# Two attentions of a transformer kernel: turns, weighing, key side and copies put in new orders

## The chip, the cores and the metric

The kernel runs on one core of one Trainium2 chip. The metric is device time in microseconds (us) for one execution, median of several runs. TensorE multiplies matrices into PSUM banks (eight, of 128 x 512 fp32), VectorE and ScalarE work on PSUM and SBUF, and SyncE (SP) issues all transfers, in one list.

## The reference

Two layers on x of 8 x 512 x 128 (8 sequences, 512 positions, 128 channels), 16 heads of width 8, so 128 heads of 512 x 512 scores in each attention:

```python
# layer 0: attention with relative positions at both sides
scores = einsum(Q, K) * scale + take(einsum(Q, pos_key) * scale, rel_pos) + swap(take(einsum(K, pos_query) * scale, p2c_pos))
ctx = softmax(scores) @ V;  x = layernorm(x + ctx @ Wo.T + bo)
# layer 0: gated feed-forward with a one-step shift; x = layernorm(x + ...)
# layer 1: attention with shifted sinusoid positions
scores = (Q K^T + u K^T + rel_shift(Q r^T + v r^T)) / sqrt(dk)
ctx = softmax(scores) @ V;  x = layernorm(x + ctx @ Wo + bo)
# layer 1: feed-forward 128 -> 512 -> 512 -> 512 -> 128; x = layernorm(x + ...)
```

## The kernel before

The program has five stages, one after the other with small overlaps: an opening that makes stacked queries, keys and values; the first attention (`rel` is true); a mixing stage; the second attention (`rel` is false); a closing stage with the last feed-forward.

In both attentions the work goes head by head. The order on each engine is written out by hand; nothing is planned at run time. A step works on head j's turns and, ahead of it, on scores, exponentials and corrections of later heads. Eight steps are unrolled in a loop; the first four and the last steps stand outside. Four heads are a group. The pieces of a step, four of each kind, one for each tile of 128 queries (or, for turns, keys):

- S, `score_tile` (L821 to L827), TensorE: a score tile of 128 x 512, 6 tiles ahead in the first attention, 7 in the second. It waits until the exponential has emptied its bank (four score banks). In the first attention a last small part goes to a shared bank `other` and waits for the mask M of the tile before.
- T, `turn` (L842), TensorE: four transposes of the head's exponentials into a bank. In the first attention turns 0 and 3 use bank 5, which the key side also uses, and turns 1 and 2 use bank 6, which the correction also uses; in the second they alternate.
- W, `weigh` (L855), TensorE: sums of values for the group before, for one quarter of the keys, four matmuls over the whole width of 512. Its first quarter waits for the copies of all four heads and for the copy of the group before out of the bank `cbank`.
- K, `key_side` (L741), TensorE, first attention: the key-side product for head j+7, which needs that head's stack `a_stks`. C, `correction` (L748, L749): for head j+5. In the second attention `edge` (L722) for head j+5 instead.
- M, `mix` (L908), F, `finish` (L920), X, `row_max` (L928), VectorE: mask (first attention only), added band, and negated maximum of a tile. `key_out` (L755) copies K's result, `edge_out` (L933) that of the edge.
- E, `exp_tile` (L980), P, `copy_turned` (L987), ScalarE: exponential of a tile (4 tiles ahead in the first attention, 5 in the second), and the copy of a turn. `corr_out` (L761) copies the correction, `group_out` (L993) the summed group, in one step of four.
- SyncE, `sync_step`: for each head of the first attention the key side is written to a DRAM buffer (L634) and read back skewed (L640), the correction likewise (L646, L652), and the stack of head j+8 is loaded in two transfers (L608, L609), in the order L634, L646, L652, L608, L609, L640. In the last step of a group come after L609 a table and offsets (L621, L628, L629), and at the end the store of the group and a load of values (L671, L673).

The orders before, by engine:

```
first attention    TensorE  S T W  S T K  S T  S T C
                   VectorE  M X F  M X F key_out  M X F  M X F
                   ScalarE  E P  E P (group_out)  E P  E P corr_out
second attention   TensorE  S T W  S T edge  S T  S T
                   VectorE  F X  F X  F X  F X edge_out
                   ScalarE  E P  E P (group_out)  E P  E P
```

Of the kernel before, what the change touches and what calls it, by code (L numbers as in the profile page):

```python
# [21 lines left out]
B, T, C = 8, 512, 128  # L22
H = 16
DH = C // H
NT = T // 128
NHEAD = B * H
# [38 lines left out]
def build(nc, t):  # L65

    top = ExitStack()
    with top:
# [430 lines left out]
        def attention(layer):  # L499
# [289 lines left out]
            def program(block, before, after):  # L789
# [56 lines left out]
                def weigh(pe, h, k):  # L846
# [15 lines left out]
                def tensor_step(pe, i, j, left, weighed=True):  # L862
                    own = Head(i, j)
                    for k in range(NT):
                        if left >= (k + score_ahead) // NT:
                            score_tile(pe, *ahead(i, j, k, score_ahead))
                        turn(pe, own, k)
                        if k == 0 and weighed:
                            weigh(pe, Head(i, j - j % GROUP - GROUP), j % GROUP)
                        if not rel and k == 1 and left >= CORR_AHEAD:  # L870
                            pe.wait_ge(corr_copied, BASE + own.n + CORR_AHEAD)
                            edge(pe, Head(i, j + CORR_AHEAD), corr_bank)
                        if rel and k == 1 and left >= KEY_AHEAD:
                            pe.wait_ge(copied, BASE + 4 * own.n + 1)
                            key_side(pe, Head(i, j + KEY_AHEAD), key_bank)
                    if rel and left >= CORR_AHEAD:
                        pe.wait_ge(copied, BASE + 4 * own.n + 3)
                        correction(pe, Head(i, j + CORR_AHEAD))

                @block.tensor  # L880
                def _(pe):
# [16 lines left out]
                    for k in range(NT):  # L898
                        weigh(pe, Head(loops, FIRST + last - GROUP), k)
# [34 lines left out]

                @block.vector
                def _(v):
# [11 lines left out]
                    def vector_step(i, j, left):  # L948
                        for k in range(NT):

                            if left >= (k + score_ahead) // NT:
                                if rel:
                                    mix(v, *ahead(i, j, k, score_ahead))
                                else:
                                    finish(v, *ahead(i, j, k, score_ahead))
                            if left >= (k + score_ahead - 1) // NT:
                                row_max(v, *ahead(i, j, k, score_ahead - 1))
                            if rel and left >= (k + score_ahead) // NT:
                                finish(v, *ahead(i, j, k, score_ahead))
                            if not rel and k == 3 and left >= CORR_AHEAD:  # L960
                                edge_out(v, Head(i, j + CORR_AHEAD))
                            if rel and k == 1 and left >= KEY_AHEAD:
                                key_out(v, Head(i, j + KEY_AHEAD), key_bank)

                    for j in range(FIRST):
                        vector_step(0, j, NHEAD)
# [3 lines left out]
                    for j in range(last):  # L970
                        vector_step(loops, FIRST + j, last - 1 - j)
                        after.vector_tail(v, last - 1 - j)

# [22 lines left out]
                def _(act):  # L996
# [3 lines left out]
                    def scalar_step(i, j, left, weighed=True):  # L1000
                        own = Head(i, j)
                        for k in range(NT):
# [1032 lines left out]
```

## Time and profile before

| | |
|---|---|
| median of 3 runs | 1965.22 us (1956.04 to 1966.07) |
| profiled execution | 1965.38 us, its span 1963.2 us |
| granted clock of TensorE, mean | 0.961 |
| TensorE, VectorE, ScalarE busy | 88%, 74%, 75% of the span |
| transfers | 404.44 MB, mean 206 GB/s |
| first attention | about 97 to 860 us |
| second attention | about 1040 to 1640 us |

All times of the trace are us from the start of the span. TensorE's weight loads (PEld) overlap its matmuls (PE). An instruction's duration overlaps the start of the next one on the same engine by about 0.1 us, so the distance of two starts is the slot that one takes.

### The profile page before, as it was taken

To read this page: it belongs to the slowest core of one execution; us is meant where nothing else is said; L and a number is where in the kernel's file an instruction comes from. 1 tells how busy PE (TensorE), PEld (TensorE's weight loads), DVE (VectorE), ACT (ScalarE), POOL (GpSimd) and SP (SyncE) were. 2 spreads that over 40 slices of the span, in tenths; PEclk is the share of its full clock that TensorE was granted. 3 is DMA by queue.
4 is the path that set the end of the run, shared out by engine and by line. 5 is a ranking of instruction groups with operands and counts; after the bars stand their busy time and mean duration, and the time that the engine had idled before them with its cause. 6 is when DMAs were issued, how large, how long until landed. Compare 5 with 4: busy or idle time off the path is not lost.

```text
span 1963.2 us, 44049 instructions
## 1 busy us (share of the span) xinstructions
PE 1728.0 (88%) x11694; PEld 1040.9 (53%) x11694; DVE 1446.4 (74%) x3501; ACT 1475.8 (75%) x2605; POOL 80.2 (4%) x102
## 2 busy tenths in 40 slices
PE   5479999999999999977767999999999989999998
PEld 2145555555555555545444655655666544545454
DVE  5568888888888888876977888888888873244322
ACT  4458888888888888876878999999999974232221
POOL 0000000000000000003520000000000000000000
PEclk8679999999999999998978999999999989999999
DMA  6788888888888888865999777777777771001000
GB/s 207 281 249 256 268 265 261 263 263 266 264 266 265 264 259 264 259 183 158 342 338 297 217 213 210 213 212 214 210 214 213 209 211 44 21 27 37 21 6 11
DMA packets 414359, 404.44 MB, mean 206 GB/s; under 512 B 36969, under 2 KB 334561, under 8 KB 414177
## 3 DMA queue, kind: packets, MB, share of 16 engines
q1 hardware_dynamic: 414305, 403.80, 67.3%
q8 instruction: 24, 0.39, 0.1%
q14 instruction: 30, 0.25, 0.0%
HBM read 226.89 MB, written 176.30 MB: 205 GB/s over the span
## 4 chain that ended last, share of the span: by engine, by line
PE 48%; issue 13%; ACT 11%; DVE 9%; SPq 8%; DMA 6%; POOL 0%; DVEq 0%; ACTq 0%; POOLq 0%
PE bank L842 12%; PE bank L1847 11%; PE bank L855 9%; ACT a_probt L987 5%; PE bank L821 4%; DVE a_negmax L928 3%; DMA a_stks<-stack 3%; ACT a_prob L980 3%; DVE a_keyside L755 2%; DVE bank L908 2%; PE bank L823 2%; PE bank L1839 1%; PE bank L1840 1%; PE bank L1868 1%; PE bank L722 1%
## 5 line engine op out<-in xcount | busy, mean ns | idle before, releaser
L980 ACT ACTIVATE a_prob<-bank,a_negmax 128x512 f32<-128x512 f32 x1024 | 738.2, 721 | 44.7 <-DVE a_negmax L928 43.2
L928 DVE TENSOR_REDUCE a_negmax<-bank 128x1 f32<-128x512 f32 x1024 | 698.3, 682 | 0.2 <-issue 0.2
L842 PE MATMUL bank<-ident,a_prob 128*128 128x128 f32 x4096 | 646.5, 281 | 56.8 <-ACT a_probt L987 49.0
L987 ACT COPY a_probt<-bank 128x512 f32<-128x512 f32 x1024 | 619.5, 605 | 97.4 <-PE bank L842 85.6
L842 PEld LDWEIGHTS bank<-ident,a_prob 128*128 128x128 f32 x4096 | 451.5, 142 | 174.9 <-issue 70.7
L920 DVE TENSOR_TENSOR bank<-bank,a_band 128x128 f32<-128x128 f32 (+3 forms) x1024 | 349.5, 341 | 81.6 <-PE bank L823 66.5
L821 PE MATMUL bank<-a_stks 74*128 74x192 bf16 (+7 forms) x1024 | 324.9, 317 | 31.5 <-ACT a_prob L980 29.4
L855 PE MATMUL bank<-a_probt,a_vs 128*32 128x512 f32 x2048 | 275.3, 612 | 12.8 <-ACT a_probt L987 12.8
L821 PEld LDWEIGHTS bank<-a_stks 74*128 74x128 bf16 (+1 forms) x1024 | 100.2, 98 | 260.0 <-ACT a_prob L980 215.0
L908 DVE COPY_PREDICATED bank<-a_mask,bank 128x128 f32<-128x128 uint32 (+1 forms) x512 | 139.4, 272 | 112.0 <-PE bank L827 109.7
L823 PE MATMUL bank<-a_stks 74*128 74x320 bf16 (+5 forms) x768 | 201.8, 263 | 0.0
L1913 DVE TENSOR_TENSOR d_drop<-bank,d_s 128x128 f32<-128x128 f32 x32 | 7.1, 283 | 170.4 <-PE bank L1868 170.4
L748 PE MATMUL bank<-ident,a_sheared 128*128 128x128 f32 x512 | 106.5, 285 | 19.4 <-DMA a_sheared<-shear_a 15.0
L827 PE MATMUL bank<-a_stks 74*128 74x128 bf16 (+1 forms) x512 | 110.4, 216 | 10.9 <-DVE bank L908 2.7
L1847 PE MATMUL bank<-d_ha,d_h1T 128*128 128x512 f32 x256 | 112.3, 592 | 0.0
L1847 PE MATMUL bank<-d_hb,d_h2T 128*128 128x512 f32 x256 | 111.2, 592 | 0.0
L755 DVE COPY a_keyside<-bank 128x512 f32<-128x512 f32 x128 | 87.2, 681 | 24.8 <-PE bank L741 24.4
L749 PE MATMUL bank<-a_tabs,a_stks 65*128 65x128 bf16 x512 | 97.5, 225 | 0.0
L761 ACT COPY a_corr<-bank 128x512 f32<-128x512 f32 x128 | 76.4, 597 | 23.2 <-DMA shear_b<-a_corr 11.9
L748 PEld LDWEIGHTS bank<-ident,a_sheared 128*128 128x128 f32 x512 | 74.3, 145 | 34.7 <-issue 21.5
L1898 ACT ACTIVATE d_hb<-bank,d_fs 128x512 f32<-128x512 f32 x32 | 22.0, 687 | 90.6 <-PE bank L1847 90.6
L1903 ACT ACTIVATE d_hc<-bank,d_fs 128x512 f32<-128x512 f32 x32 | 22.0, 687 | 87.6 <-PE bank L1847 87.6
(178 smaller groups left out, 1622.7 us busy)
## 6 DMA issues: line engine op xcount, KB each, us to landing
a_band<-shear_b SPq DMA_DIRECT2D x128, 512.0 KB, 4.9
shear_a<-a_keyside SPq DMA_DIRECT2D x128, 256.0 KB, 3.7
a_sheared<-shear_a SPq DMA_DIRECT2D x128, 256.0 KB, 3.7
shear_b<-a_corr SPq DMA_DIRECT2D x128, 256.0 KB, 2.8
shear_e<-a_corr SPq DMA_DIRECT2D x128, 256.0 KB, 2.2
a_band<-shear_e SPq DMA_DIRECT2D x128, 256.0 KB, 3.1
a_stks<-stack SPq DMA_DIRECT2D x256, 96.0 KB, 3.0
a_stks<-stack SPq DMA_DIRECT2D x384, 48.0 KB, 2.5
```

The costliest lines, as they stand in the source:

```text
L748: pe.matmul(corr_bank[:, q], sheared[h.slot % 4][:, q], ident[:, :], is_transpose=True, start=True, stop=False)
L755: v.tensor_copy(keyside[h.slot % 4][:, :], source[:, :]).then_inc(key_copied, 1)
L821: last = pe.matmul(score[:, 0:c], k[:, qlo, q], k[:, keys, 0:c], start=True, stop=True)
L823: last = pe.matmul(score[:, c:T], k[:, qhi, q], k[:, keys, c:T], start=True, stop=True)
L842: last = pe.transpose(turned_bank[k][:, n * 128:(n + 1) * 128], prob[h.slot % 2][:, n, k * 128:(k + 1) * 128], ident[:, :])
L855: pe.matmul(cbank[32 * j:32 * j + VW, :], vs[g][:, at:at + VW], probt[h.slot + j][:, k, :], start=(k == 0), stop=(k == NT - 1)).then_inc(p ...
L908: v.copy_predicated(score[:, a:e], mask[:, 0:e - a], other[:, 0:e - a]).then_inc(fixed, 1)
L920: v.tensor_tensor(score[:, a:e], score[:, a:e], band[h.slot % bands][:, n, w:w + e - a], ALU.add).then_inc(added, 1)
L928: v.tensor_reduce(negmax[h.slot % 2][:, n:n + 1], score[:, :], AX.X, ALU.max, negate=True).then_inc(maxed, 1)
L980: nc.scalar.activation(prob[h.slot % 2][:, n, :], score[:, :], ACT.Exp, bias=negmax[h.slot % 2][:, n:n + 1]).then_inc(exped, 1)
L987: nc.scalar.copy(probt[h.slot][:, k, :], turned_bank[k][:, :]).then_inc(copied, 1)
L1847: last = pe.matmul(dst[:, :], w[:, k, 128 * m:128 * m + 128], src[:, k, :], start=(k == 0), stop=(k == KH - 1))
```

## The change

Both attentions get orders of their own in place of a loop over the four pieces. By engine:

```
first attention    TensorE  S T  S T K W  T S  T S C
                   VectorE  M X  M F F X key_out X  M F  M X F
                   ScalarE  P E  P E E  P E  P (group_out) corr_out
second attention   TensorE  S T T  S W S  T T  S edge
                   VectorE  F X  F X (group copy)  F X  F X edge_out
                   ScalarE  E P P E  E P P E
```

The copy of the summed group in the second attention moves from ScalarE to VectorE. `weigh` gets an argument for columns, which always is the whole width. SyncE's list is not changed. The core of the diff (the VectorE and ScalarE orders in it are those of the lines above):

```diff
-                def weigh(pe, h, k):
+                def weigh(pe, h, k, cols):
...
-                        pe.matmul(cbank[32 * j:32 * j + VW, :], vs[g][:, at:at + VW], probt[h.slot + j][:, k, :],
-                                  start=(k == 0), stop=(k == NT - 1)).then_inc(pv_mm, 1)
+                        part = pe.matmul(cbank[32 * j:32 * j + VW, cols], vs[g][:, at:at + VW], probt[h.slot + j][:, k, cols],
+                                         start=(k == 0), stop=(k == NT - 1 and cols.stop == T))
+                        if cols.stop == T:
+                            part.then_inc(pv_mm, 1)
...
+                def shifted_tensor_step(pe, i, j, left, weighed=True):
                     own = Head(i, j)
-                    for k in range(NT):
-                        if left >= (k + score_ahead) // NT:
-                            score_tile(pe, *ahead(i, j, k, score_ahead))
-                        turn(pe, own, k)
-                        if k == 0 and weighed:
-                            weigh(pe, Head(i, j - j % GROUP - GROUP), j % GROUP)
-                        if not rel and k == 1 and left >= CORR_AHEAD:
-                            pe.wait_ge(corr_copied, BASE + own.n + CORR_AHEAD)
-                            edge(pe, Head(i, j + CORR_AHEAD), corr_bank)
-                        if rel and k == 1 and left >= KEY_AHEAD:
-                            pe.wait_ge(copied, BASE + 4 * own.n + 1)
-                            key_side(pe, Head(i, j + KEY_AHEAD), key_bank)
-                    if rel and left >= CORR_AHEAD:
+                    score_ahead_of(pe, i, j, left, 0)
+                    turn(pe, own, 0)
+                    score_ahead_of(pe, i, j, left, 1)
+                    turn(pe, own, 1)
+                    if left >= KEY_AHEAD:
+                        pe.wait_ge(copied, BASE + 4 * own.n + 1)
+                        key_side(pe, Head(i, j + KEY_AHEAD), key_bank)
+                    if weighed:
+                        weigh(pe, Head(i, j - j % GROUP - GROUP), j % GROUP, slice(0, T))
+                    turn(pe, own, 2)
+                    score_ahead_of(pe, i, j, left, 2)
+                    turn(pe, own, 3)
+                    score_ahead_of(pe, i, j, left, 3)
+                    if left >= CORR_AHEAD:
                         pe.wait_ge(copied, BASE + 4 * own.n + 3)
                         correction(pe, Head(i, j + CORR_AHEAD))
+
+                def edged_tensor_step(pe, i, j, left, weighed=True):
+                    own = Head(i, j)
+                    score_ahead_of(pe, i, j, left, 0)
+                    turn(pe, own, 0)
+                    turn(pe, own, 1)
+                    score_ahead_of(pe, i, j, left, 1)
+                    if weighed:
+                        weigh(pe, Head(i, j - j % GROUP - GROUP), j % GROUP, slice(0, T))
+                    score_ahead_of(pe, i, j, left, 2)
+                    turn(pe, own, 2)
+                    turn(pe, own, 3)
+                    score_ahead_of(pe, i, j, left, 3)
+                    if left >= CORR_AHEAD:
+                        pe.wait_ge(corr_copied, BASE + own.n + CORR_AHEAD)
+                        edge(pe, Head(i, j + CORR_AHEAD), corr_bank)
...
+                def edge_group_out(v, h):
+
+                    v.wait_ge(pv_mm, BASE + 16 * (h.use(GROUP) + 1))
+                    v.wait_ge(out_written, BASE + 16 * h.use(GROUP))
+                    v.tensor_copy(outs[:, :], cbank[:, :]).then_inc(out_copied, 1)
...
-                    group_out(act, Head(loops, FIRST + last - GROUP))
+                    if rel:
+                        group_out(act, Head(loops, FIRST + last - GROUP))
```

## Rows read from the trace of the kernel before

**Rows 1.** Busy time by stretch: us, busy (x instructions) by engine, PEclk, DMA share, GB/s.

```profile
500.00:700.00 200.00, 186.50 (x1481) 115.63 (x1480) 170.43 (x438) 173.85 (x312) 0.00 (x0) 1.00 0.86 263
...
1300.00:1500.00 200.00, 188.34 (x1561) 119.49 (x1558) 176.67 (x403) 196.63 (x368) 0.00 (x0) 1.00 0.73 212
```

**Rows 2.** Waits, 200 to 800 us: who waited for whom, us in total, times, longest.

```profile
PE bank L741 <- DMA a_stks<-stack: 6.2, 10, 1.2
```

**Rows 3.** Timeline, one step of the first attention: start, us, engine, line, tiles, idle before.

```profile
201.84 0.63 PE L842 MATMUL bank<-ident,a_prob 128*128 128x128 f32 x4 [0.18 <-ACT a_probt L987]
...
202.40 1.06 PE L855 MATMUL bank<-a_probt,a_vs 128*32 128x512 f32 x8
...
203.39 0.39 PE L821 MATMUL bank<-a_stks 74*128 74x512 bf16 x1
...
203.65 0.63 PE L842 MATMUL bank<-ident,a_prob 128*128 128x128 f32 x4
...
203.96 0.23 DVE L908 COPY_PREDICATED bank<-a_mask,bank 128x64 f32<-128x64 uint32 x1 [0.92 <-PE bank L827]
...
204.12 0.38 PE L741 MATMUL bank<-a_stks,a_tabs 65*128 65x512 bf16 x1
...
204.20 0.35 SPq L609 DMA_DIRECT2D a_stks<-stack  x1
...
204.96 0.68 DVE L755 COPY a_keyside<-bank 128x512 f32<-128x512 f32 x1
...
206.48 0.27 PE L748 MATMUL bank<-ident,a_sheared 128*128 128x128 f32 x1
...
207.17 0.35 PE L821 MATMUL bank<-a_stks 74*128 74x448 bf16 x1
...
207.78 0.63 PE L842 MATMUL bank<-ident,a_prob 128*128 128x128 f32 x4 [0.18 <-ACT a_probt L987]
```

**Rows 4.** Timeline, copies of the summed groups in the first attention (L993).

```profile
162.29 0.59 ACT L993 COPY a_outs<-bank 128x512 f32<-128x512 f32 x1
...
786.04 0.59 ACT L993 COPY a_outs<-bank 128x512 f32<-128x512 f32 x1
...
809.82 0.59 ACT L993 COPY a_outs<-bank 128x512 f32<-128x512 f32 x1
...
834.53 0.59 ACT L993 COPY a_outs<-bank 128x512 f32<-128x512 f32 x1
```

**Rows 5.** Chain of waits after 216 us, and the instruction it ends in.

```profile
217.15 5.13 DMA a_stks<-stack
...
222.40 0.39 PE L741 MATMUL bank<-a_stks,a_tabs 65*128 65x512 bf16 x1 [0.27 <-DMA a_stks<-stack]
```

**Rows 6.** Transfers issued at 312.7, 337.9 and 792.4 us (L609): count, KB, us to landing.

```profile
a_stks<-stack SPq DMA_DIRECT2D x1, 48.0 KB, 6.1
...
a_stks<-stack SPq DMA_DIRECT2D x1, 48.0 KB, 3.6
...
a_stks<-stack SPq DMA_DIRECT2D x1, 48.0 KB, 5.0
```

**Rows 7.** Timeline, second attention: ScalarE's pair of copy and exponential, group copies, weighing.

```profile
1108.43 0.78 ACT L980 ACTIVATE a_prob<-bank,a_negmax 128x512 f32<-128x512 f32 x1
...
1109.02 0.67 ACT L987 COPY a_probt<-bank 128x512 f32<-128x512 f32 x1
...
1109.48 0.80 ACT L980 ACTIVATE a_prob<-bank,a_negmax 128x512 f32<-128x512 f32 x1
...
1114.88 0.63 ACT L993 COPY a_outs<-bank 128x512 f32<-128x512 f32 x1
...
1117.78 1.07 PE L855 MATMUL bank<-a_probt,a_vs 128*32 128x512 f32 x8 [0.44 <-ACT a_probt L987]
...
1132.89 0.63 ACT L993 COPY a_outs<-bank 128x512 f32<-128x512 f32 x1
...
1150.81 0.63 ACT L993 COPY a_outs<-bank 128x512 f32<-128x512 f32 x1
```

More of the change, by code:

```diff
@@ L898, in _ @@
                     for k in range(NT):
-                        weigh(pe, Head(loops, FIRST + last - GROUP), k)
+                        weigh(pe, Head(loops, FIRST + last - GROUP), k, slice(0, T))
                 def mix(v, h, n):
@@ L946, in _, with mix_ahead_of @@
                             row_max(v, *ahead(0, 0, 0, n - 1))
[L948 to L963, printed above, removed]
+                    def mix_ahead_of(i, j, left, k):
+                        if left >= (k + score_ahead) // NT:
+                            mix(v, *ahead(i, j, k, score_ahead))
@@ new lines, in edged_vector_step @@
+                    def edged_vector_step(i, j, left, weighed=True):
+                        finish_ahead_of(i, j, left, 0)
+                        max_ahead_of(i, j, left, 0)
+                        finish_ahead_of(i, j, left, 1)
+                        max_ahead_of(i, j, left, 1)
+                        if weighed and j % GROUP == GROUP - 1:
+                            edge_group_out(v, Head(i, j - j % GROUP - GROUP))
+                        finish_ahead_of(i, j, left, 2)
+                        max_ahead_of(i, j, left, 2)
+                        finish_ahead_of(i, j, left, 3)
+                        max_ahead_of(i, j, left, 3)
+                        if left >= CORR_AHEAD:
+                            edge_out(v, Head(i, j + CORR_AHEAD))
@@ L972, in _ @@
                         after.vector_tail(v, last - 1 - j)
+                    if not rel:
+                        edge_group_out(v, Head(loops, FIRST + last - GROUP))
                 def exp_tile(act, h, n):
@@ L998, in _, with exp_ahead_of, shifted_scalar_step, edged_scalar_step @@
                         exp_tile(act, *ahead(0, 0, 0, n))
[L1000 removed]
+                    def exp_ahead_of(i, j, left, k):
+                        if left >= (k + exp_ahead) // NT:
+                            exp_tile(act, *ahead(i, j, k, exp_ahead))
+                    def shifted_scalar_step(i, j, left, weighed=True):
                         own = Head(i, j)
[L1002 to L1009 removed]
+                        copy_turned(act, own, 0)
+                        exp_ahead_of(i, j, left, 0)
+                        copy_turned(act, own, 1)
+                        exp_ahead_of(i, j, left, 1)
+                        exp_ahead_of(i, j, left, 2)
+                        copy_turned(act, own, 2)
+                        exp_ahead_of(i, j, left, 3)
+                        copy_turned(act, own, 3)
+                        if weighed and j % GROUP == GROUP - 1:
+                            group_out(act, Head(i, j - j % GROUP - GROUP))
+                        if left >= CORR_AHEAD:
+                            corr_out(act, Head(i, j + CORR_AHEAD))
+                    def edged_scalar_step(i, j, left, weighed=True):
+                        own = Head(i, j)
+                        exp_ahead_of(i, j, left, 0)
+                        copy_turned(act, own, 0)
+                        copy_turned(act, own, 1)
+                        exp_ahead_of(i, j, left, 1)
+                        exp_ahead_of(i, j, left, 2)
+                        copy_turned(act, own, 2)
+                        copy_turned(act, own, 3)
+                        exp_ahead_of(i, j, left, 3)
+                    scalar_step = shifted_scalar_step if rel else edged_scalar_step
                     for j in range(FIRST):
```

35 lines of the change are left out of this document (27 added, 8 removed).

## The prediction

> **What bounds the kernel now.** I read the busy shares by stretch first: they show two long regular stretches, the two attentions, and a last stretch that the change does not touch. In the first attention no engine is full: TensorE 93%, VectorE 85%, ScalarE 87%, DMA 86%, at a granted clock of 1.00 [rows 1]. In the second ScalarE is full: 196.6 of 200 us [rows 1]. Next the waits, for what closes the first attention's loop: now and then TensorE's key-side product waits for a load of the head's stack (10 times, 6.2 us) [rows 2]. Then one step by the timeline, 201.84 to 207.78: 5.94 us [rows 3]. The loop in it: turn 0 at 201.84, the weighing at 202.40, and only then the score tile at 203.39; VectorE sat idle 0.92 us for that tile's end (mask at 203.96), so its key-side copy starts at 204.96 though the key-side product started at 204.12 and took 0.38 us; the fourth tile's last part, the fourth turn, its copy and the next turn 0 (207.78, released by a copy, 0.18 us idle) follow from there. The 1 us of weighing stands where VectorE has nothing to do.
>
> Groups of four heads take more than 4 x 5.94 = 23.8 us: 24.01 on average (162.29 to 834.53, 28 groups), the last two 23.78 and 24.71 [rows 4]. The chain says what the excess is: after a group step SyncE is behind. The stack load is issued at 217.15, 9.37 us after the group step's turn 0 (207.78), lands 5.13 us later, and the key-side product of the step after the next starts at 222.40, released by it [rows 3, 5]. In such a step that product stands 2.28 us after turn 0, so it may start at 2 x 5.94 + 2.28 = 14.2 us; the load landed at 14.5.
>
> **The first attention, part by part.** Nothing is removed; TensorE's order becomes S T S T K W T S T S C. Its own pace from the rows [rows 3]: a turn followed by a small product 0.47 (203.65 to 204.12), four of them 1.9; the weighing 0.99 (202.40 to 203.39); the correction 0.69 (206.48 to 207.17); the four tiles 0.26 (203.39 to 203.65) to 0.35 each, 1.3; the key side 0.2 to 0.3. Sum 5.15 to 5.25. Now each wait, with t = 0 at turn 0. Turn 0 ends 0.65, its copy (0.59, now first on ScalarE) ends 1.28, so K goes at 1.33. W at 1.55 to 2.54, where ScalarE copies the second turn (ends 2.35) and VectorE does mask, maximum and band of two tiles: the wait of 0.92 is covered. VectorE: K's copy after the third of its pieces starts 2.5 and ends 3.2; turn 3 wants it at 3.36. The masks M2 and M3 follow S2 and S3 (about 3.7 and 4.5), the maximum after them ends 5.3, before the exponential that needs it at 5.9. The band add F2 now stands directly behind its own mask M2 and waits for its completion: 0.1 us, in a gap before S3 ends, so nothing. ScalarE: copy, exp, copy, exp, exp, copy, exp, copy, correction copy; 4 x 0.59 + 5 x 0.46 = 4.7 us (the slots of 1108.43 to 1109.02 and 1109.02 to 1109.48) [rows 7], with the last turn's copy ending at 5.1; the next turn 0 can start at 5.2. The group copy, moved from the second turn to the step's end, pushes the correction's copy by 0.46 in one step of four and the next turn 1 by 0.1. So all three engines allow about 5.27 us, 21.1 us a group against 23.8: 0.67 us a head.
>
> What is late next is the load. K moves from 2.28 to 1.33 us after turn 0, and the steps are shorter. What queues behind its wait on TensorE is W, both remaining turns, S2, S3 and C: everything. SyncE's list is untouched, and in the group step it runs without a pause (correction copy, then band, two stack loads, table, offsets, store, values): the load of the following step is issued 9.4 us after the group step's turn 0 in the new order too. Its landing took 5.1, 6.1, 3.6 and 5.0 us in four groups [rows 5, 6], mean 4.95. K may start at 2 x 5.27 + 1.33 = 11.9, the load is there at 9.4 + 4.95 = 14.35: a stall of 2.45 us a group (bounds: 1.1 with 3.6, 3.6 with 6.1). Nothing catches it up. Group: 21.1 + 2.45 = 23.55 against 24.01, 0.46 less; some 30 groups: **14 us** off. The gain's ends: 0.67 x 120 = 80 us plus the old stalls' 7 if landings shrink to nothing that binds, and below nothing in the last rival. I take 14 since landing times are measured and SyncE's order stays.
> In a plain step the load is issued 2.36 us after turn 0 (204.20) [rows 3] and K of the next step wants it at 5.27 + 1.33 = 6.6: 4.2 us for a landing. That holds with 3.6, not with 5.1; after the stall there is 2.5 us of slack, so I count nothing.
>
> On landing times the Trainium skill (DMA: Bandwidth & Descriptors, "Anatomy of one DMA") gives, as a fit for transfers of the other descriptor path, about 2.0 us plus bytes over 436 GB/s. The trace does not agree for this load: 3.6 to 6.1 us with DMA 86% busy [rows 1, 6]. By that fit 48 KB would be there in 2.1 us, K would never wait, and the total would come out as in the first rival.
>
> **The second attention.** ScalarE makes a pair of exponential and copy in 1.05 us (1108.43 to 1109.48), 4.2 a step, plus the group's copy, another slot of 0.46 [rows 7]. Groups take 18.01 (1114.88 to 1132.89) and 17.92 (1132.89 to 1150.81) [rows 7]: 4 x 4.22 = 16.9, 0.5 for the copy, 0.6 for a hole. The hole: the group's copy delays the next turn's copies, the weighing that needs them waits 0.44 (1117.78) [rows 7] with everything behind it. The change takes the group's copy from ScalarE and gives it to VectorE, after the weighing's new place. VectorE's busy time goes from 88% of 4.49 us [rows 1] = 3.97 to 3.97 + 0.68/4 = 4.1 us a step: below 4.22. In the group step its copy (0.6) pushes the next mask-free add and maximum; an exponential then comes 0.15 to 0.2 us late. TensorE: busy at most 94% of 4.49 = 4.23 [rows 1], with modelled ends; turn, turn, tile, weighing, tile, turn, turn, tile, edge leaves it 4.0 to 4.1. The weighing now has two turns and a tile between itself and the last copy it waits for, so the 0.44 goes. Pairs E E and P P do not stand in the trace; I take the sum of the two slots, 1.05, as in an alternating pair; if each had the copy's or the exponential's slot it would be 0.92 or 1.18. The last exponential of a step writes the buffer that turn 3 reads, and now stands behind both copies, so that wait is over. Group: 16.9 + 0.2 = 17.1 against 17.97, 0.87 less; about 30 groups: **26 us** (ends: 0 and 36, the latter with no late exponential and no hole).
>
> The `cols` argument always holds the whole width: no cost. The last group's copy goes to VectorE, beside other work: 0.7 us at most.
>
> Sum against the profiled execution, 1965.38 us (span 1963.2, 2.2 around it; the median of the three runs is 1965.22, so both stand alike): 1965.4 - 14 - 26 = 1925. I forecast **1925 us**, its own range 1900 to 1945.
>
> **Rivals.** First, the loads land in time: DMA queues less where it is drained evenly. For it: half the groups have no stall now (23.78) [rows 4]. Against it: 86% of 24.0 us is 20.6 us of DMA work a group, in 21.1 us. Time: 1965.4 - 78 - 26 = 1861.
> Second, the loads take the whole gain of the first attention: stall 2.9 us a group, which landings of 5.4 us would make (5.1 and 6.1 were seen, and DMA is denser). Only the second attention gains: 1939.
> Third, neither gains: in the second attention two turns back to back cost more than a turn and a tile (no row shows them; 0.63 us each, the duration of one, instead of 0.45 brings TensorE to 4.5 us a step), and the first is as in the second rival. Time 1965.
> Fourth, the other side. The plain steps too wait for their load: with K at 1.33, a step is as long as issue and landing allow, 2.36 + L - 1.33. With L = 4.0 it is 5.03 and does not bind; with 5.13 it is 6.16, more than today's 6.00. Slower in total by over 10 us needs 6.3 us, so L of 5.3 or more in every step; at 5.4 it is 6.43: 0.43 x 120 = 52 later, 26 gained, 1991. For it: SyncE issues nothing earlier and DMA fills up. Against it: a longer step empties the queue again.
>
> **How the numbers follow.** Forecast 0.52; loads in time 0.10; second attention alone 0.16; neither 0.12; every step waits 0.10. Against 0.5% (10 us, about what a measurement of this kernel can tell from no change): faster 0.52 + 0.10 + 0.16 = 0.78, same 0.12, slower 0.10. The range runs from 1868, which leaves out half of the first rival and more, to 1966, which leaves out the last: 0.82 inside.
>
> **What would show it.** In the changed profile: VectorE's wait for the tile behind the weighing (0.92) gone; plain steps of 5.2 to 5.4 us between turn 0s; TensorE's key side waiting for the stack load in nearly every group, 1 to 4 us, in total 50 to 90 us; group copies 22.5 to 24.5 us apart. In the second attention no 0.44 before the weighing, ScalarE still over 97% busy, groups 17.0 to 17.3 us apart, with VectorE's copy of the sums in them. It is wrong if plain steps stay at 5.9 (then a walk of mine missed a wait), if the key side hardly waits, or if TensorE's steps in the second attention exceed 4.3 us.

## The result

The changed kernel takes 1975.49 us (median of 20 runs, 1962.34 to 1993.38), the kernel before 1962.03 us (20 runs, 1955.85 to 1968.74): the ratio is 1.0074, 95% interval 1.0057 to 1.009. It is slower by about 14 us where 1925 was forecast, and outside the range. In the experiments below a ratio is always to the kernel before, measured beside it on the same chip. "Groups" are the mean distance of two copies of a summed group, in us. A group step is the step of each four in which the group's copy stands; the stalled step is the second one behind it; the others are called plain.

The profiled execution took 1989.61 us (span 1987.8, mean granted clock 0.931) against 1965.38 (1963.2, 0.961), 24.6 us more of span. This execution is one of the slower ones, 14 us above the median of the 20, so the losses read from its trace are at the upper end. In the 20 runs the time follows the granted clock: 1962.34 us at 0.946, 1975.06 at 0.939, 1993.38 at 0.930. By landmarks: the last copy of a correction in the first attention moved from 856.1 to 889.2, so 33.1 us are lost up to there; 4.4 more are lost before the second attention; the second attention wins 13.3 back; the end loses 0.4.

The busy times by stretch, changed kernel (us, then busy time and instructions of TensorE (PE), its weight loads (PEld), VectorE (DVE), ScalarE (ACT) and POOL, then granted clock, DMA share, GB/s), answer to [rows 1]:

```profile
500.00:700.00 200.00, 181.29 (x1396) 115.40 (x1395) 163.78 (x414) 161.69 (x295) 0.00 (x0) 0.91 0.82 250
...
1300.00:1500.00 200.00, 196.19 (x1607) 120.67 (x1605) 186.10 (x423) 196.84 (x368) 0.00 (x0) 1.00 0.76 218
```

In the first attention every engine did less in 200 us than before, and the clock is 0.91 where it was 1.00. The second has its old clock and did more in its 200 us. ScalarE is 98% busy there, as before.

The copies of the summed groups, changed kernel, first attention (ScalarE) and second (VectorE), the first and the 29th of 32, and the second and the 27th of 32, answer to [rows 4, 7]:

```profile
168.33 0.60 ACT L1057 COPY a_outs<-bank 128x512 f32<-128x512 f32 x1
...
868.59 0.61 ACT L1057 COPY a_outs<-bank 128x512 f32<-128x512 f32 x1
```

```profile
1134.30 0.69 DVE L965 COPY a_outs<-bank 128x512 f32<-128x512 f32 x1
...
1570.89 0.69 DVE L965 COPY a_outs<-bank 128x512 f32<-128x512 f32 x1
```

A group takes (868.59 - 168.33) / 28 = 25.01 us in the first attention (before 24.01), and (1570.89 - 1134.30) / 25 = 17.46 us in the second (before 17.97).

The waits of the key-side product, 200 to 800 us, changed kernel (who waited for whom, us in total, times, longest), answer to [rows 2]:

```profile
PEld bank L741 <- issue: 50.4, 27, 3.5
...
PE bank L741 <- DMA a_stks<-stack: 34.9, 13, 3.2
```

A row for the weight load and a row for the matmul: they overlap, and the first counts at least once for each of the 24 groups in the window. Before, the same two rows had 15 waits of 10.5 us in all (longest 1.4) and 10 of 6.2 (longest 1.2). Some rows name a copy or "issue" in place of the load; there too the load lands just as the wait ends (351.89 + 4.3 us for the key side at 356.26, 403.07 + 4.3 for the one at 407.49). The chain of waits runs through the same load (start, us, what), as in [rows 5]:

```profile
427.60 5.18 DMA a_stks<-stack
...
432.91 0.61 PE bank L741
...
433.52 1.87 PE bank L855 x8
```

The weighing is the line to look at: its row says 1.87 us. The timeline (start, us, engine, line, operation, idle time before) of the same kernel, at a stalled step (330.47), at two plain steps (349.23, 399.89), at a second stalled step (403.87 to 409.76) and at a third (784.48), answers to [rows 3]:

```profile
330.47 0.61 PE L741 MATMUL bank<-a_stks,a_tabs 65*128 65x512 bf16 x1 [3.22 <-DMA a_stks<-stack]
...
331.01 1.94 PE L855 MATMUL bank<-a_probt,a_vs 128*32 128x512 f32 x8
...
349.23 0.39 PE L741 MATMUL bank<-a_stks,a_tabs 65*128 65x512 bf16 x1 [0.57 <-DMA a_stks<-stack]
...
349.57 1.06 PE L855 MATMUL bank<-a_probt,a_vs 128*32 128x512 f32 x8
...
399.89 0.39 PE L741 MATMUL bank<-a_stks,a_tabs 65*128 65x512 bf16 x1
...
400.22 1.06 PE L855 MATMUL bank<-a_probt,a_vs 128*32 128x512 f32 x8
...
403.07 0.35 SPq L609 DMA_DIRECT2D a_stks<-stack  x1
...
403.87 0.61 PE L842 MATMUL bank<-ident,a_prob 128*128 128x128 f32 x4
...
407.49 0.48 PE L741 MATMUL bank<-a_stks,a_tabs 65*128 65x512 bf16 x1 [2.21 <-issue]
...
407.89 1.94 PE L855 MATMUL bank<-a_probt,a_vs 128*32 128x512 f32 x8
...
409.76 1.12 PE L842 MATMUL bank<-ident,a_prob 128*128 128x128 f32 x4
...
784.48 0.39 PE L741 MATMUL bank<-a_stks,a_tabs 65*128 65x512 bf16 x1 [2.78 <-DMA a_stks<-stack]
...
784.79 1.07 PE L855 MATMUL bank<-a_probt,a_vs 128*32 128x512 f32 x8
```

Directly behind a wait of 3.22 or 2.21 us the weighing (L855) takes 1.94 us; behind none, or 0.57 us, it takes 1.06. The turn behind it at 409.76 takes 1.12 instead of 0.66, as at 401.22 in the step before. But behind a wait of 2.78 us, at 784.48, the weighing takes 1.07 too. The granted clock, read in half microseconds over 200 to 800 us, falls during or behind 20 of the 24 stalls, for 3.5 to 7 us each, and stays at 1.00 at four. The shortest wait with a fall is 1.53 us, the longest without one 2.78, so the length of the wait alone does not decide. The granted clock in the three pieces around the stall at 407.49:

```profile
401.00:406.00 5.00, 4.28 (x39) 3.16 (x35) 4.72 (x13) 4.60 (x9) 0.00 (x0) 1.00 0.95 277
...
407.50:411.00 3.50, 3.50 (x15) 1.41 (x16) 1.29 (x2) 0.08 (x1) 0.00 (x0) 0.52 0.99 293
...
411.00:413.00 2.00, 2.00 (x22) 1.66 (x20) 1.44 (x5) 1.64 (x4) 0.00 (x0) 0.99 0.41 155
```

It is 1.00 (2.4 GHz) ahead of the stall, 0.52 (1.2 GHz) in the 3.5 us of dense work behind it, 0.99 after that.

In the second attention two waits are new or larger (1100 to 1600 us, changed kernel): VectorE's band add waits for its transfer, and an exponential waits for a maximum.

```profile
DVE bank L946 <- DMA a_band<-shear_e: 16.7, 28, 2.4
...
ACT a_prob L1044 <- DVE a_negmax L954: 12.9, 21, 2.4
```

One such place, behind a group step: SyncE issues the read of the band, VectorE wants it, it is late, and an exponential is late behind it.

```profile
1264.89 0.38 SPq L665 DMA_DIRECT2D a_band<-shear_e  x1
...
1268.64 0.82 ACT L1044 ACTIVATE a_prob<-bank,a_negmax 128x512 f32<-128x512 f32 x1
...
1269.26 0.30 DVE L946 TENSOR_TENSOR bank<-bank,a_band 128x128 f32<-128x128 f32 x1 [0.99 <-DMA a_band<-shear_e]
...
1270.19 0.69 ACT L1044 ACTIVATE a_prob<-bank,a_negmax 128x512 f32<-128x512 f32 x1 [0.72 <-DVE a_negmax L954]
```

### The profile page after: what moved, and what is told of

Its sections match the earlier page's. It is cut to its first block, busy times and chain, and to the rows that moved or that the text cites. A ratio compares the mean times of both kernels' runs of the same rounds, so it can differ in the third digit from the quotient of the medians.

```text
span 1987.8 us, 44062 instructions
## 1 busy us (share of the span) xinstructions
PE 1747.4 (88%) x11694; PEld 1054.3 (53%) x11694; DVE 1472.9 (74%) x3533; ACT 1450.3 (73%) x2573; POOL 80.0 (4%) x102
## 4 chain that ended last, share of the span: by engine, by line
PE 53%; SPq 15%; DMA 12%; issue 8%; DVE 6%; ACT 5%; POOL 0%; DVEq 0%; ACTq 0%; POOLq 0%
PE bank L842 14%; PE bank L1934 11%; PE bank L855 8%; DMA a_band<-shear_e 5%; PE bank L821 4%; DMA a_stks<-stack 4%; PE bank L748 3%; PE bank L823 2%; DVE a_negmax L954 2%; PE bank L741 2%; ACT a_probt L1051 1%; PE bank L1926 1%; PE bank L1927 1%; PE bank L1955 1%; PE bank L827 1%
## 5 line engine op out<-in xcount | busy, mean ns | idle before, releaser
L1044 ACT ACTIVATE a_prob<-bank,a_negmax 128x512 f32<-128x512 f32 x1024 | 699.3, 738 | 33.8 <-DVE a_negmax L954 32.5
L1051 ACT COPY a_probt<-bank 128x512 f32<-128x512 f32 x1024 | 595.6, 629 | 123.7 <-PE bank L842 117.6
L842 PE MATMUL bank<-ident,a_prob 128*128 128x128 f32 x4096 | 619.5, 286 | 12.8 <-ACT a_probt L1051 10.0
L842 PEld LDWEIGHTS bank<-ident,a_prob 128*128 128x128 f32 x4096 | 459.3, 145 | 185.4 <-ACT a_probt L1051 89.9
L946 DVE TENSOR_TENSOR bank<-bank,a_band 128x128 f32<-128x128 f32 (+3 forms) x1024 | 340.5, 344 | 71.7 <-DMA a_band<-shear_e 25.9
L821 PE MATMUL bank<-a_stks 74*128 74x192 bf16 (+7 forms) x1024 | 329.9, 322 | 33.9 <-ACT a_prob L1044 30.3
L855 PE MATMUL bank<-a_probt,a_vs 128*32 128x512 f32 x2048 | 290.2, 642 | 0.8 <-ACT a_probt L1051 0.4
L748 PE MATMUL bank<-ident,a_sheared 128*128 128x128 f32 x512 | 113.2, 298 | 23.2 <-DMA a_sheared<-shear_a 18.3
L741 PE MATMUL bank<-a_stks,a_tabs 65*128 65x512 bf16 x128 | 53.4, 417 | 84.8 <-DMA a_stks<-stack 39.6
L827 PEld LDWEIGHTS bank<-a_stks 74*128 74x128 bf16 x512 | 51.3, 100 | 76.4 <-DVE bank L934 53.0
```

Of the source, the lines that this page charges most:

```text
L748: pe.matmul(corr_bank[:, q], sheared[h.slot % 4][:, q], ident[:, :], is_transpose=True, start=True, stop=False)
L821: last = pe.matmul(score[:, 0:c], k[:, qlo, q], k[:, keys, 0:c], start=True, stop=True)
L827: last = pe.matmul(other[:, 0:e - a], k[:, qhi, q], k[:, keys, a:e], start=True, stop=True)
L842: last = pe.transpose(turned_bank[k][:, n * 128:(n + 1) * 128], prob[h.slot % 2][:, n, k * 128:(k + 1) * 128], ident[:, :])
L855: part = pe.matmul(cbank[32 * j:32 * j + VW, cols], vs[g][:, at:at + VW], probt[h.slot + j][:, k, cols], start=(k == 0), stop=(k == NT - 1 ...
L946: v.tensor_tensor(score[:, a:e], score[:, a:e], band[h.slot % bands][:, n, w:w + e - a], ALU.add).then_inc(added, 1)
```

## The experiments

Two theories stood against each other for the first attention: that the stall at the key side costs its own length and slows the clock behind it, and that the new orders are in themselves no faster (a wait that the prediction's walk through the step missed). For the second attention the rivals were ScalarE's new order and the late band.

### Each attention alone

e1_second_only has the old orders in the first attention, e2_first_only in the second:

```diff
-tensor_step = shifted_tensor_step if rel else edged_tensor_step
+tensor_step = old_tensor_step if rel else edged_tensor_step       # e1
+tensor_step = shifted_tensor_step if rel else old_tensor_step     # e2
 # likewise vector_step and scalar_step; the second attention's group copy follows its orders
```

> Old orders in the first attention, new orders in the second alone. Theory: the first attention of the changed kernel is what costs; in its profile the second attention's groups are 17.5 us apart instead of 17.97, so this kernel should be some 13 to 15 us faster than before (about 1948 us). Rival: the second attention's gain is lost at its ends or needs the first one's, then within 5 us of before (1962).

> New orders in the first attention alone, old ones in the second. Theory: groups of the first attention 25.1 us apart instead of 24.0, plus the slower start: 25 to 35 us slower than before (about 1990 us), granted clock in that stretch near 0.90. Rival: the loss sits in the second attention or between the two, then about 1962.

e1: 1951.16 us, ratio 0.9946 (0.9933 to 0.9959), groups 23.91 and 17.45 us. e2: 1991.66 us, 1.0157 (1.0141 to 1.0172), groups 24.69 and 17.97, mean clock 0.939. So the second attention gives about 10 us, somewhat less than the 13 to 15 expected, and the first costs about 30, as expected, though at a clock of 0.95 in its stretch where 0.90 was expected. Their product, 1.010, is a little above the 1.0074 of both together. The changed kernel's own runs lie 31 us apart, those of before 13. As time and clock go together in those runs, a number of falls that differs from run to run would make such a spread (20 in the trace above, 15 in e2's over the same 600 us); this was not tested. e2's stretch:

```profile
300.00:500.00 200.00, 180.53 (x1431) 114.00 (x1431) 168.37 (x424) 166.88 (x303) 0.00 (x0) 0.95 0.86 262
```

### The load of the stack at the top of SyncE's list

```diff
                 if rel:
+                    if left >= LOAD_AHEAD:
+                        hold(sp, maxed, 4 * (n + 1))
+                        head_load(sp, Head(i, j + LOAD_AHEAD))
                     if left >= CORR_AHEAD + 1:
                         shear_a_write(sp, Head(i, j + CORR_AHEAD + 1))
...
-                    if left >= LOAD_AHEAD:
-                        hold(sp, maxed, 4 * (n + 1))
-                        head_load(sp, Head(i, j + LOAD_AHEAD))
```

> The changed kernel with one edit: SyncE issues the two stack loads at the top of each step of the first attention instead of behind the band read. Theory (the key side waits for the load after each group step, and the clock falls behind that wait): the load of the step behind a group step is issued about 2.5 us earlier, the stall of 2 to 3 us goes to under 1, the clock stays at 1.00, groups of 21.5 to 22.5 us; about 75 to 100 us faster than the changed kernel, 1880 to 1900 us. Rival (the transfers as a whole are the limit, whichever comes first): another transfer, the band or the sheared key side, is late instead and the groups stay at 24 us or more, 1950 us or more.

e3 is the changed kernel with this edit, e10 the kernel before with it.

> The kernel before with old orders everywhere and one edit: the stack loads at the top of SyncE's step in the first attention. Theory (the old order was bound by its own loop through the weighing, and the late load cost only 0.3 us a group): 5 to 12 us faster than before, 1950 to 1957 us, groups of 23.7 us. Rival (the late load was the bound already and the new orders add nothing of their own): 1900 us or less.

e3: 1893.5 us, 0.9653 (0.9637 to 0.967). e10: 1957.54 us, 0.9976 (0.9965 to 0.9988), groups 23.76. e3's stretch and its first and last group copy of the first attention:

```profile
300.00:500.00 200.00, 195.72 (x1637) 125.95 (x1632) 191.42 (x484) 188.01 (x345) 0.00 (x0) 1.00 0.94 293
```

```profile
167.40 0.61 ACT L1057 COPY a_outs<-bank 128x512 f32<-128x512 f32 x1
...
771.94 0.62 ACT L1057 COPY a_outs<-bank 128x512 f32<-128x512 f32 x1
```

The clock is 1.00, DMA is at 0.94, and a group takes 604.54 / 28 = 21.59 us; the forecast without a stall was 21.1. e3's time is in the range expected, e10's gain of 5 us at the low end of it. So the new orders do nearly what the walk said once the stack load is on time. What is left, 0.49 us a group, has a candidate in e3's trace (200 to 750 us, 25 groups): the correction waits for the key side that is read back, 0.38 us a group.

```profile
PE bank L748 <- DMA a_sheared<-shear_a: 9.5, 18, 1.1
```

The first attention alone: new orders without the earlier load cost 30 us (e2), the earlier load without new orders gives 5 (e10), both give 58 (e3's 68 less the second attention's 10). Neither part shows what they are worth together.

### The same stall, with the engine kept at work

e4 adds two products of 128 x 512 into the key side's bank, ahead of the key side, in the step that stalls. Nothing reads them. All waits stay.

```diff
                         pe.wait_ge(copied, BASE + 4 * own.n + 1)
+                        if weighed and own.slot % GROUP == 1:
+                            for _ in range(2):
+                                pe.matmul(key_bank[:, :], ident[:, :], probt[own.slot][:, 0, :], start=True, stop=True)
                         key_side(pe, Head(i, j + KEY_AHEAD), key_bank)
```

> The changed kernel with two products added ahead of the key side in the one step of four that waits for its load; their results are overwritten at once. They add 1.7 us of TensorE work inside a wait of 2 to 4 us. Theory (a long wait of TensorE lowers its clock, and the steps behind it run at 1.2 GHz for some us): the weighing behind the key side takes 1.06 us instead of 1.94, granted clock of the stretch 0.97 or more, 30 to 45 us faster than the changed kernel, about 1935 to 1945 us. Rival (the wait alone costs, the clock's fall is no consequence of it): no change or up to 10 us slower where the wait is shorter than the added work, 1975 to 1985 us.

e4: 1948.02 us, 0.9942 (0.9924 to 0.9961), groups 23.58. The two products, the key side and the weighing of such a step (timeline, TensorE), and the stretch:

```profile
317.04 1.98 PE L879 MATMUL bank<-a_probt,ident 128*128 128x512 f32 x4
...
320.39 0.39 PE L741 MATMUL bank<-a_stks,a_tabs 65*128 65x512 bf16 x1 [1.37 <-DMA a_stks<-stack]
...
320.71 1.07 PE L855 MATMUL bank<-a_probt,a_vs 128*32 128x512 f32 x8
```

```profile
300.00:500.00 200.00, 194.88 (x1545) 121.42 (x1542) 176.58 (x449) 174.56 (x318) 0.00 (x0) 1.00 0.88 268
```

TensorE is given 1.98 us of useless work a group, the key side still waits 1.37 us for its transfer, and the kernel is some 27 us faster than the changed one, a little short of the 30 to 45 expected. The weighing is back at 1.07 us behind every such wait, and the clock does not fall once between 150 and 760 us. The load lands no sooner (4.1 us after its issue in the median, 4.0 in the changed kernel). This takes the length of the stall and the clock apart: 23.58 is close to what the forecast had for the stall alone (23.55), and of the 1.4 us above it in the changed kernel all but some tenths are the clock's. The tenths may be a longer wait: the changed kernel's 24 stalls average 2.3 us, and 23.58 is 2.0 above e3's 21.59.

### The weighing ahead of the key side

```diff
                     turn(pe, own, 1)
+                    if weighed:
+                        weigh(pe, Head(i, j - j % GROUP - GROUP), j % GROUP, slice(0, T))
                     if left >= KEY_AHEAD:
                         pe.wait_ge(copied, BASE + 4 * own.n + 1)
                         key_side(pe, Head(i, j + KEY_AHEAD), key_bank)
-                    if weighed:
-                        weigh(pe, Head(i, j - j % GROUP - GROUP), j % GROUP, slice(0, T))
```

> The changed kernel with one edit: in the first attention the weighing stands before the key side instead of behind it. Theory (the key side waits for a load that comes 2 to 3 us late in one step of four, and everything queued behind it waits): the weighing's 1.0 us fills the wait, the stall goes to 1 to 2 us, the clock mostly stays up; groups of 22.5 to 23.5 us instead of 25.1, about 1905 to 1930 us. Rival (the key side's copy, now late for turn 3, costs 0.3 us or more in every step): groups of 23.5 us or more, 1935 us or more.

e7: 1932.69 us, 0.9835 (0.9814 to 0.9855), groups 23.10, clock 1.00 from 300 to 700 us and two falls before that. The groups are in the range expected, the time is 3 us above it. The order takes the place of part of the stall, but in every step turn 3 now waits for VectorE's copy of the key side, and an exponential for its maximum (200 to 750 us):

```profile
PEld bank L842 <- DVE a_keyside L755: 35.3, 96, 0.4
...
ACT a_prob L1044 <- DVE a_negmax L954: 24.3, 96, 0.4
```

Some 0.37 and 0.25 us a step. With the late load this order is 43 us faster than the change's; with the load on time it was not run, and these waits speak for the change's order there.

### The second attention

e5 has the old orders in the first attention, keeps the new orders of TensorE and VectorE in the second, and lets ScalarE alternate there again; it is to be compared with e1:

```diff
-    exp_ahead_of(i, j, left, 0)
-    copy_turned(act, own, 0)
-    copy_turned(act, own, 1)
-    exp_ahead_of(i, j, left, 1)
... 
+    for k in range(NT):
+        exp_ahead_of(i, j, left, k)
+        copy_turned(act, own, k)
```

> Old orders in the first attention; in the second the new orders of TensorE and VectorE with the group copy on VectorE, but ScalarE alternating exponential and copy as before. Compare with the second attention alone (1951 us, groups 17.5 us). Theory (two exponentials back to back take 0.66 us each, an alternating pair 1.05, so ScalarE's new order costs 0.16 us a step and ScalarE is the bound): groups of 17.0 to 17.2 us, about 1940 us. Rival (VectorE or TensorE sets the 17.5): groups stay at 17.4 to 17.6, 1950 us.

e5: 1975.03 us, 1.0052 (1.0036 to 1.0069), groups 18.35 in the second attention. Neither the expectation nor its rival came true. With two turns back to back the next pair waits for a copy that the alternating order gives late (timeline, TensorE, e5):

```profile
1221.12 0.66 PE L843 MATMUL bank<-ident,a_prob 128*128 128x128 f32 x4 [0.35 <-ACT a_probt L1088]
...
1225.58 0.66 PE L843 MATMUL bank<-ident,a_prob 128*128 128x128 f32 x4 [0.28 <-ACT a_probt L1088]
```

ScalarE's paired slots were never dear (timeline, ScalarE, e1; x2 is two instructions back to back):

```profile
1218.67 1.29 ACT L1081 ACTIVATE a_prob<-bank,a_negmax 128x512 f32<-128x512 f32 x2
...
1219.82 1.10 ACT L1088 COPY a_probt<-bank 128x512 f32<-128x512 f32 x2
...
1220.76 1.33 ACT L1081 ACTIVATE a_prob<-bank,a_negmax 128x512 f32<-128x512 f32 x2
```

From 1218.67 to 1220.76 are two exponentials and two copies: 2.09 us, 1.045 a pair, where the forecast took 1.05.

e6 is the kernel before with nothing but the group copy on VectorE in the second attention, e8 is e3's first attention with e6's second.

> The kernel before with one edit: in the second attention the group copy is on VectorE, behind the maximum of the second piece; all orders old. Theory (the copy's slot on ScalarE and the hole behind it were all there was to win; ScalarE is full): groups of 17.0 to 17.2 us instead of 17.97, about 1938 us, faster than all new orders of the second attention (1951). Rival (the hole of 0.44 us before the weighing needs the weighing's new place): groups of 17.4 to 17.6, about 1950 us.

> First attention as changed with the stack loads at the top of SyncE's step (1893.5 us with the new second attention); second attention with old orders and the group copy on VectorE. Theory, as for the group copy alone: 10 to 13 us less than 1893.5, so 1880 to 1884 us. Rival, as there: 1893 us.

e6: 1962.06 us, 0.9997 (0.9986 to 1.0007), groups 17.88. e8: 1903.5 us, 0.9697 (0.9679 to 0.9716), about 10 us behind e3. Both expectations fell. In e6 the slot leaves ScalarE, and the hole stays:

```profile
1223.62 0.68 DVE L984 COPY a_outs<-bank 128x512 f32<-128x512 f32 x1
...
1225.21 0.69 ACT L1081 ACTIVATE a_prob<-bank,a_negmax 128x512 f32<-128x512 f32 x1 [0.27 <-DVE a_negmax L973]
...
1226.52 1.06 PE L856 MATMUL bank<-a_probt,a_vs 128*32 128x512 f32 x8 [0.80 <-ACT a_probt L1088]
```

VectorE's copy delays a maximum, the exponential 0.27 us, and the weighing waits 0.80 us for a turn's copy. So the copy's new engine alone does not take the hole away. In the changed kernel, where the weighing has its new place as well, no weighing waits for a turn's copy (1100 to 1600 us); no run moves the weighing alone.

e9 and e11 ask whether the late band can be had earlier by reading it ahead of the next write; e9 on top of e3, e11 with the stack's load behind L634 instead of at the top.

```diff
                 else:
-                    if left >= CORR_AHEAD:
-                        edge_write(sp, Head(i, j + CORR_AHEAD))
...
                         edge_read(sp, Head(i, j + CORR_AHEAD - 1))
+                    if left >= CORR_AHEAD:
+                        edge_write(sp, Head(i, j + CORR_AHEAD))
```

> The changed kernel with the stack loads at the top of SyncE's step in the first attention (1893.5 us) and, in the second, the skewed band read ahead of the edge write in SyncE's step, so that it no longer stands behind the wait for the edge copy. Theory (the second attention's 17.5 us instead of the 17.1 forecast are the band add that waits for this read in or after a group step, and the exponential behind it): no wait of VectorE for the band read, groups of 16.9 to 17.2 us, 8 to 14 us less, about 1882 us. Rival (the group copy on VectorE alone makes exponentials late): groups stay at 17.4 or more, 1890 us or more.

> As the load at the top with the band read first, but the stack loads stand behind the key side's write, so that write is no longer 1 us later. Theory: the load of the step behind a group step is issued 0.6 us later than at the top, its slack shrinks from about 1 us to 0.5, some groups stall by less than 1 us, the clock stays at 1.00: within 8 us of the load at the top, on either side. Rival (a threshold of the clock is met again): 15 us or more slower than the load at the top.

e9: 1903.35 us, 0.9693 (0.9673 to 0.9712), groups 21.57 and 17.89. e11: 1908.77 us, 0.9728 (0.9698 to 0.9757), groups 22.01 and 17.88. e9 missed: from 1100 to 1500 us the band is waited for 41 times, 20.6 us, in place of e3's 24 times, 11.0 us. SyncE now waits for the write's landing, and the write of the next head stands behind that read (e9):

```profile
SPq L598 <- DMA shear_e<-a_corr: 38.6, 65, 1.5
```

e11 is 5 us behind e9, the kernel that it differs from by the load alone, and 15 behind e3, where the expectation allowed 8 and its rival began at 15; 10 of them e9 has too. Its correction waits 17.1 us for the key side that is read back (200 to 750 us; e9 10.7), and its clock falls once, during such a wait of 2.03 us that ends at 355.07, in a group of 26.05 us.

e12 leaves the order of write and read, and issues every other group's store and load of values one step later, behind the band's read, in place of ahead of the next step's write:

```diff
                         edge_read(sp, Head(i, j + CORR_AHEAD - 1))
+                    if weighed and j == 2 * GROUP:
+                        group_store(sp, Head(i, j - 2 * GROUP), left + 1 >= GROUP * (vslots - 1))
...
-                if weighed and j % GROUP == GROUP - 1:
+                if weighed and j % GROUP == GROUP - 1 and (rel or j != 2 * GROUP - 1):
```

> The changed kernel with the stack loads at the top (1893.5 us), and in the second attention the store of every other group and its load of values issued one step later, behind that step's band read instead of ahead of its edge write; the other groups stay as they are, so that both kinds stand in one trace. Theory (what the second attention lost against the forecast is the band read that SyncE issues 1.1 us late behind a group's store): about half of the waits of VectorE for the band read go (27 or so in the stretch become some 14), groups behind a moved store are 0.3 to 0.5 us shorter, 1886 to 1890 us in all. Rival (the group copy on VectorE alone makes them): both kinds of groups stay at 17.5 us and the waits at their number, 1892 to 1896 us.

e12: 1888.38 us, 0.9624 (0.9603 to 0.9645), as expected, the fastest of all, and faster than both kernels; its interval overlaps that of e3. Its groups of the second attention take 17.26 us, and every other one is shorter, as the edit is in every other one: the group behind a moved store takes 17.05 us, the other 17.37, over the 24 from 1069.50 to 1482.49. The waits for the band and for the maximum, 1100 to 1500 us, of e3 and then of e12:

```profile
DVE bank L946 <- DMA a_band<-shear_e: 11.0, 24, 1.1
...
ACT a_prob L1044 <- DVE a_negmax L954: 5.9, 14, 0.8
```

```profile
DVE bank L948 <- DMA a_band<-shear_e: 8.9, 24, 1.2
...
ACT a_prob L1046 <- DVE a_negmax L956: 1.4, 4, 0.8
```

The band is waited for as often and for little less, which is short of the expectation; but the waits that reach ScalarE, the full engine, fall from 5.9 to 1.4 us. Where the edit acts, the group comes out at the forecast's 17.1. So where SyncE issues the store and the load of values is what the second attention lacked. Whether they cost by delaying the issue of the band's read or by sharing the DMA engines with it, these runs do not separate. The other half of the groups was not changed, and that case stays untried.

## Why the prediction was wrong

**The step that failed** is "Group: 21.1 + 2.45 = 23.55", in the first attention. It took the stall at the key side as time in which nothing happens, and all work behind it at the granted clock of 1.00 that the rows of before show [rows 1]. The stall came where it was put: group step begun at 393.13, load issued at 403.07, stalled step begun at 403.87, key side at 407.49, so 14.36 us after the group step's start (forecast 14.35) and 2.21 us late (forecast 2.45). But the work behind it ran at 0.52: the stalled step lasts from 403.87 to 412.89, 9.02 us, which is 5.27 for the step, 2.21 for the wait and 1.5 for the clock, of which the weighing (1.94 for 1.06) and the next turn (1.12 for 0.66) already make 1.3. 23.55 + 1.5 = 25.05; measured 25.01. That the two meet so closely is in part luck: the step's share was 21.1 for e3's 21.59, and the 1.5 is from one stall, where four of 24 had no fall and eight a fall twice as long. Over some 30 groups 1.5 us are 45 us, and that turns 14 us won into 30 lost. e4 shows it as a cause and not a companion: the same transfer, more work, clock 1.00, 23.58 us. The kernel before had waits of the same kind with its clock at 1.00, at most 1.2 us long in [rows 2] and 1.4 in the row of the weight load; nothing at its key side showed a wait of over 2 us inside the dense stretch, and the forecast did not ask what one does.

Here a page bears on it. The Trainium skill (TensorE: Matmul & The Clock Gate, "HAM oscillation — how this bites in real kernels") describes a kernel in which each wait for a transfer between bursts of matmuls throttles TensorE again, so that the next burst starts slow. The trace agrees in kind, with 0.52 behind 2.21 us, but not at every wait: four of 24 have no fall. With 1.5 us a group more the second rival (1939, a stall of 2.9 us) would have stood at 1939 + 45 = 1984, on the slow side.

**Right in the first attention:** the walk of the step. Plain steps last 5.2 to 5.5 us (weighings at 389.59, 394.76 and 400.22; forecast 5.2 to 5.4). VectorE's wait for the tile behind the weighing has all but gone, from 86.1 us in 100 waits before (200 to 800 us) to 11.9 in 33 in e3 (200 to 750). Without the stall a group takes 21.59 (e3) for the 21.1 reckoned. The forecast had no term for the key side that is read back; e3's 0.38 us a group there would be most of the 0.49, which no run tests. The stall of nearly every group, 50 to 90 us in all, was seen: 50.4 us in 24 groups are 63 in 30. Group copies "22.5 to 24.5 us apart" were not. That "SyncE's order stays" was the change's real limit was right, and e3 prices it at 82 us against the changed kernel.

**Second attention: mechanism right, size off.** The term "26 us" measured about 10 (e1), 0.51 us a group for 0.87. The weighing waits for no copy of a turn any more, ScalarE's slots cost 2.09 us for two pairs against 2.10. What was mis-sized is "an exponential comes 0.15 to 0.2 us late": it is 12.9 us in 21 waits (0.6 each), 0.45 us for each of the 28 or so groups in that stretch, the one at 1270.19 being 0.72 us, behind a band that landed 0.99 us after VectorE wanted it. The forecast looked at SyncE's lateness after a group step in the first attention and not in the second, where the same store and load of values stand ahead of the band. e12, which moves them in every other group, brings those groups to 17.05 us, the forecast's 17.1.

**Rivals.** That the loads are on time was worked out as 1861; e3, which makes them so, is at 1893.5. Of the 32 us of difference 11 are the second attention's shortfall (0.36 us in each of 30 groups) and 15 the first's (0.49). The rival's own sum took 78 us where 80 and the old stalls' 7 were given before it, so it should have read 1852. The fourth, that plain steps too wait for their load, happened only here and there (0.57 us at 349.23), though it had the right sign. The changed kernel was slower than before by another mechanism, the clock, which no rival had. The 6 us by which the first group copy was late already (168.33 for 162.29; 164 to 166 in the other traces with the old orders) and the 4.4 us between the attentions stay open.

## What to carry to other kernels

Before an in-order engine's work is put in a new order, list for each transfer its issue, its landing and the new moment of need: here one load in four came 2.3 us late on average, and two lines moved in SyncE's list were worth 82 us. Where TensorE waits inside dense work for as long as it did here (1.5 us and more), price the wait as its own length plus, most of the time (20 of 24 here), some microseconds of the work behind it at half the clock. Try it with filler products, which nothing reads: where more work makes a kernel faster, the clock was the cost. An order judged together with one late transfer is misjudged: neither the new orders alone (1.0074) nor the load alone (0.9976) pointed to 0.9653.

## What the runs showed of the hardware

- The granted clock fell to 0.52 behind a single wait of 2.21 us, with dense work at 1.00 ahead of it, and stayed there for about 3.5 us of dense work. In the changed kernel it fell at 20 of 24 such waits, the shortest 1.53 us; it did not fall behind 0.57 us, nor at one of 2.78 us. With 1.98 us of products ahead of the wait it never fell, at waits of up to 1.5 us (e4).
- The wait need not be for that load: in e11 the clock fell during one of 2.03 us for another transfer.
- With transfers at 0.94 of the 16 engines' time (e3) the first attention ran faster than at 0.86 (the kernel before): the share of DMA was no bound here, the order of its issues was.
- In the second attention an edit that only lets a read go ahead of a write lengthened groups from 17.44 to 17.89 us (e9 against e3); SyncE then stood 38.6 us in 65 waits for landings, in 400 us.
